# Attention-only batches in another order: scores by pairs of heads, all row maxima first, low-rank products in two row groups and a quad earlier

## The chip, the core and the metric

The kernel runs on one core of one Trainium2 chip. A core has five engines that run side by side, each its own list of instructions in order: TensorE (PE in the tables, its weight loads PEld), VectorE (DVE), ScalarE (ACT), GpSimd (POOL) and SyncE (SP), which here only issues DMAs. They wait for one another on semaphores. The metric is the device time of one execution in microseconds (us).

## The reference

Two layers act on x of shape (8, 256, 512): 8 batches of 256 tokens. Only layer 0 is touched by the change:

```python
# layer 0, attention (16 heads of 32), then an FFN with 4-bit weights and a low-rank addition
xn = rms_norm(x, g_norm) * (1 + scale) + shift          # scale, shift = emb @ W_emb + b_emb
q, k, v = heads(xn @ W_qkv);  q, k = rms_norm(q, g_q), rms_norm(k, g_k)
attn = softmax(q @ k.T * 32 ** -0.5);  o = attn @ v
x1 = o + o @ W_out
w_up = (w_up_q - 7.5) * repeat(w_up_scale, 64)
x2 = relu(x1 @ w_up.T + b_up + x1 @ w_up_lora_a @ w_up_lora_b)
x = x + x2 @ w_down.T + b_down + x2 @ w_down_lora_a @ w_down_lora_b
# layer 1: a scan over 256 tokens (4 stages each), then a mixture of experts
```

## The kernel before

Layer 0 takes the eight batches one after the other. The FFN trails the attention by `LAG` = 3 batches, so batches 0, 1 and 2 are attention only, and batches 3 to 7 carry an FFN of an earlier batch between the attention's instructions (`ffn` is true there). While batches 0 and 1 run, the FFN's weights are made: 16 pieces of 1024 columns, 8 in each batch, by this chain for each piece h. SyncE loads its codes and scales (L238 to L248) into one of two staging buffers, once piece h-2 has left it; VectorE forms (code - 7.5) * scale (`scaled`, L760); TensorE makes the low-rank product a @ b, two matmuls of 16 rows by 512 columns into the banks D[0] and D[1] (`lora`, L555), once piece h-1 has been added; VectorE adds the product (`restore`, L767, two instructions); ScalarE takes the high half in f16 (`weights_high`, L416); GpSimd takes the rest (`weights_low`, L320). In all three batches VectorE also takes maxima over 512-wide parts of layer 1's weights (`part_max`, L772): 12 in batch 1, 36 in batch 2.

A batch has two stretches. In the first, TensorE projects q, k and v (L614, L592) and VectorE scales them (L837, L838); four pieces are made beside it. In the second, four quads c of four heads each go through: scores of the quad into the four banks X[0] to X[3] (L633, one head in each 32-row group of TensorE); row maxima on VectorE (`row_max`, L846, one for a head); exponentials on ScalarE (`exps`, L485, two halves for a head); transposes on TensorE back into the head's bank (L639); a copy to SBUF on VectorE (`turned`, L855). The next quad's scores wait until all four copies are done (L629). Then `weighted(c)` makes the spread inverse sums and the products with v (L652, L657), ScalarE and VectorE gather them (L491, L852). After quad 3 comes the output projection (L686), which waits for the last gather.

VectorE's list in a quad before: the maxima of heads 0, 1 and 2, the gather of the last quad, the copy of head 0, the `restore` of a piece (c > 0), the maximum of head 3, the copies of heads 1 and 2, the reciprocal (L849), the copy of head 3, `scaled` of the next piece. In quad 2 it ends with the next batch's L804, in quad 3 the next batch's L809 stands ahead of the `restore`. The product of the piece for which quad c > 0 has its `restore` stands on TensorE behind `weighted(c-1)`; the eighth piece's stands behind `weighted(3)`, ahead of the output projection.

## Time and profile before

| | |
|---|---|
| median of 3 runs | 2866.41 us (2859.16 to 2866.79) |
| the profiled execution's own time | 2869.92 us |
| its span, first to last instruction | 2868.2 us |
| mean granted TensorE clock | 0.969 of full speed |
| TensorE busy | 2742.7 us (96%) |
| VectorE busy | 1752.6 us (61%) |
| ScalarE busy | 1118.3 us (39%) |
| GpSimd busy | 1345.3 us (47%) |

All times inside the kernel are those of the profiled execution, counted from its first instruction. A granted clock of 1.0 is TensorE's level of 2.4 GHz, 0.5 that of 1.2 GHz; a value between them is a mean over a stretch that had both. An engine's idle time is put down to the instruction whose semaphore came last. A matmul on f32 shows as two records, one for each pass.

### The profile page before, as it was taken

What the parts mean: (1) busy time and instruction counts of PE and PEld (TensorE: products, weight loads), DVE (VectorE), ACT (ScalarE), POOL (GpSimd) and SP (SyncE); (2) the same over time, 40 slices, a digit from 0 to 9 for tenths busy, and PEclk for the clock granted to TensorE, in tenths of its full rate; (3) what the DMA queues carried; (4) which work ended last, traced back from release to release, by engine and by line L of the source; (5) the groups of instructions that cost most, each with busy time, mean ns of one, the idle gap of its engine ahead of it and who ended that gap; (6) DMA issues with size and microseconds to landing.
All of it is one profiled execution on the core that took longest, in us unless ns stands there. A gap on an engine that the chain in (4) does not pass through costs nothing.

```text
span 2868.2 us, 132456 instructions
## 1 busy us (share of the span) xinstructions
PE 2742.7 (96%) x49104; PEld 2436.5 (85%) x49104; DVE 1752.6 (61%) x6310; ACT 1118.3 (39%) x4954; POOL 1345.3 (47%) x3459
## 2 busy tenths in 40 slices
PE   7878999999899989999999999999999999999998
PEld 5545677777799979999998998998999899899987
DVE  3566566655655556666666666666666666666654
ACT  2343435654444333343333333333333333333322
POOL 1120011221156656666665665665666566566600
PEclk9888999999999979999999999999999999999999
DMA  7343344544410014444443443433444344344376
GB/s 231 96 133 121 107 154 149 173 158 150 129 48 4 4 49 129 128 128 134 130 130 125 128 128 125 130 129 125 132 128 128 125 128 129 124 133 128 119 238 202
DMA packets 140246, 364.63 MB, mean 127 GB/s; under 512 B 17536, under 2 KB 27392, under 8 KB 139520
## 3 DMA queue, kind: packets, MB, share of 16 engines
q1 hardware_dynamic: 137504, 355.55, 39.1%
q10 hardware_dynamic: 2560, 6.49, 0.7%
q8 instruction: 135, 2.21, 0.3%
q14 instruction: 47, 0.39, 0.0%
HBM read 327.50 MB, written 34.47 MB: 126 GB/s over the span
## 4 chain that ended last, share of the span: by engine, by line
PE 68%; DVE 1%; issue 1%; ACT 0%; DMA 0%; DVEq 0%; POOL 0%; ACTq 0%; POOLq 0%; SPq 0%
PE pscan L1420 14%; PE pscan L1416 13%; PE pg L1322 12%; PE pd L1373 12%; PE pu L1322 12%; PE pd L1346 2%; PE pg L1334 1%; PE prouter L1334 1%; PE pu L1334 1%; PE prouter L1434 0%; DMA wd<-w_split 0%; PE prouter L1442 0%; DVE state L1549 0%; ACT th L1229 0%; PE pd L1449 0%
## 5 line engine op out<-in xcount | busy, mean ns | idle before, releaser
L1416 PEld LDWEIGHTS pscan<-th,carry 128*128 128x128 f16 x16384 | 561.2, 96 | 38.4 <-ACT th L1229 17.5
L1416 PE MATMUL pscan<-th,carry 128*128 128x8 f16 x16384 | 559.9, 166 | 14.3 <-ACT th L1229 14.1
L1420 PE MATMUL pscan<-th,carry 128*128 128x16 f16 x16384 | 558.7, 169 | 2.4 <-DVE th L1532 1.5
L1420 PEld LDWEIGHTS pscan<-th,carry 128*128 128x128 f16 x16384 | 482.8, 96 | 4.0 <-DVE th L1532 3.5
L1229 ACT ACTIVATE th<-state 128x32 f16<-128x32 f32 x768 | 176.1, 229 | 704.4 <-DVE state L1549 704.4
L1322 PE MATMUL pg<-qh,wgu 128*128 128x256 f16 x3168 | 431.1, 276 | 14.3 <-issue 14.1
L1373 PE MATMUL pd<-hg,wd 128*128 128x256 f16 x3168 | 428.8, 274 | 2.4 <-DMA wd<-w_split 2.4
L1322 PE MATMUL pu<-qh,wgu 128*128 128x256 f16 x3168 | 425.2, 273 | 0.0
L1549 DVE TENSOR_REDUCE state<-pscan 128x32 f32<-128x96 f32 x768 | 197.9, 258 | 271.9 <-PE pscan L1420 267.5
L1322 PEld LDWEIGHTS pg<-qh,wgu 128*128 128x128 f16 x3168 | 296.0, 98 | 54.0 <-issue 15.5
L1322 PEld LDWEIGHTS pu<-qh,wgu 128*128 128x128 f16 x3168 | 293.4, 98 | 32.9
L1373 PEld LDWEIGHTS pd<-hg,wd 128*128 128x128 f16 x3168 | 277.9, 97 | 31.8 <-issue 2.7
L1544 DVE SCALAR_TENSOR_TENSOR pscan<-pscan,lin 128x32 f32<-128x32 f32 x1024 | 204.7, 200 | 127.0 <-DVE pscan L1535 19.9
L1532 DVE TENSOR_TENSOR th<-pact,th 128x32 f16<-128x32 f32 x1024 | 191.2, 187 | 119.3 <-ACT pact L1230 115.1
L1197 POOL TENSOR_TENSOR from_q<-state,carry 128x32 f32<-128x32 f32 x256 | 91.2, 356 | 245.8 <-DVE state L1549 245.8
L1191 POOL TENSOR_TENSOR from_q<-state,carry 128x64 f32<-128x64 f32 x256 | 113.1, 442 | 170.7 <-DVE state L1549 170.7
L1229 ACT ACTIVATE th<-carry 128x32 f16<-128x32 f32 x256 | 58.6, 229 | 342.0 <-DVE carry L1549 333.2
L485 ACT ACTIVATE w_emb<-l0bank,nmax 128x256 f32<-128x256 f32 x256 | 118.7, 474 | 122.1 <-DVE nmax L846 121.7
L1297 ACT ACTIVATE hg<-hp 128x256 f16<-128x256 f32 x264 | 109.8, 416 | 124.3 <-DVE hp L1594 117.5
L326 POOL TENSOR_SCALAR late<-parts_mem 128x512 f16<-128x512 f16 x33 | 51.4, 1559 | 226.8 <-DMA w_split<-late 138.2
L1594 DVE SCALAR_TENSOR_TENSOR hp<-hb,wk,gates 128x256 f32<-128x256 f32 x264 | 141.9, 538 | 18.6 <-DVE hb L1587 7.6
L1535 DVE SCALAR_TENSOR_TENSOR pscan<-pscan,state 128x32 f32<-128x32 f32 x768 | 147.6, 192 | 0.0
(225 smaller groups left out, 4730.8 us busy)
## 6 DMA issues: line engine op xcount, KB each, us to landing
wgu<-w_split SPq DMA_DIRECT2D x264, 512.0 KB, 3.5
wd<-w_split SPq DMA_DIRECT2D x264, 384.0 KB, 3.1
parts_mem<-in_w_tiles SPq DMA_DIRECT2D x159, 256.0 KB, 3.7
w_split<-parts_mem SPq DMA_DIRECT2D x99, 256.0 KB, 2.6
late<-in_w_tiles SPq DMA_DIRECT2D x39, 256.0 KB, 4.0
w_split<-late SPq DMA_DIRECT2D x33, 128.0 KB, 3.0
hid<-in_up_q SPq DMA_DIRECT2D x8, 512.0 KB, 4.3
hid<-in_up_s SPq DMA_DIRECT2D x16, 256.0 KB, 5.2
```

Source lines behind the costliest of these rows:

```text
L485: ins = act.activation(pr[:, h % HPC, qc, :], X[h % HPC][:, qc * T:(qc + 1) * T], ACT.Exp, bias=nmax[:, h % HPC, qc:qc + 1], accum_out=psu ...
L1191: pl.tensor_tensor(ms3[:], rows(state[2][:], 2), c3[:], ALU.mult).then_inc(S["pchain"], 1)
L1229: act.activation(th[:, :, 0, :], v3(src[:]), ACT.Tanh, scale=unit).then_inc(S["th_ready"], 1)
L1322: ins = mm(dst[:, 0:GT], wgu[:, slot, a, w, k, :], qh[:, q, k, :], start=(k == 0 and w == q), stop=(k == NC - 1 and w == 1))
L1373: ins = mm(pd[m // 2][:, (m % 2) * GT:(m % 2 + 1) * GT], wd[:, slot, w, m * P:(m + 1) * P], hg[:, slot, h, :], start=False, stop=False, sk ...
L1416: mm(pscan[:, 0, m * B:(m + 1) * B], clo[:, k, m * P:(m + 1) * P], th[:, k, 0, :], start=(m == 0 and k == 0), stop=False, skip_group_check ...
L1420: ins = mm(pscan[:, 0:2, m * B:(m + 1) * B], chi[:, k, m * P:(m + 1) * P], th[:, k], start=False, stop=(k == NC - 1), skip_group_check=True)
L1532: dve.tensor_tensor(th[:, :, 1, :], v3(t32), th[:, :, 0, :], ALU.subtract).then_inc(S["tl_ready"], 1)
L1535: chain(dve.scalar_tensor_tensor(cub, sq, shift, state[s][:], ALU.add, ALU.mult), False)
L1544: chain(dve.scalar_tensor_tensor(pscan[:, 2, 0:W], cub, -RK[s - 1] / 3, A[u][:, s, :], ALU.mult, ALU.add), False)
L1549: dve.tensor_reduce(nxt[:], pscan[:, 0:3, 0:W].rearrange("p a w -> p w a"), AX.X, ALU.add).then_inc(S["q_ready"], 1)
L1594: dve.scalar_tensor_tensor(hp[:], hb[:], wk[:, 4:5], g, ALU.mult, ALU.mult).then_inc(S["hp_ready"], 1)
```

## The change

In batches 0, 1 and 2 only:

- Scores are made and announced by pairs of heads: the pair of heads 0 and 1 of the next quad waits for the copies of heads 0 and 1 alone, the second pair for those of heads 2 and 3.
- VectorE has a list of its own for these batches (`attention_quad`): four maxima, then `restore` of a piece, then the four copies with the reciprocal behind the third, the gather of the last quad, `scaled` of the next piece. The fourth piece of a batch (`scaled`, `restore`, and the `part_max` that stood behind it) moves from the end of the first stretch into quad 0, behind its maxima.
- The product of piece 4 + c is made behind the transposes of quad c, so that it stands before the `restore` of quad c + 1 needs it, and the eighth piece's stands ahead of `weighted(3)`. The two matmuls of a product read two copies of the factors, at partitions 0 and 64 (or 32 and 96), so they use two different row groups of TensorE. The factors are loaded and scaled twice for it.
- ScalarE takes the four heads' exponentials in a row, with the gather copy and `weights_high` behind them.
- The low half of a batch's eighth piece is made by VectorE, between the two additions that follow the output projection, in place of GpSimd, with a semaphore of its own (`split_end`).

The kernel before and the changed one list their instructions as follows; line numbers are each one's own. VectorE in quad 1 of batch 0, before: L846 is a maximum, L852 the gather, L855 a copy, L767 `restore`, L849 the reciprocal, L760 `scaled`.

```order
L846 TENSOR_REDUCE nmax<-l0bank 128x2 x3
L852 TENSOR_TENSOR late<-l0bank,late 128x256
L855 COPY carry<-l0bank 128x512
L767 SCALAR_TENSOR_TENSOR hid<-hid,fs,l0bank 128x512 x2
L846 TENSOR_REDUCE nmax<-l0bank 128x2
L855 COPY carry<-l0bank 128x512 x2
L849 RECIPROCAL rinv<-psum_e 128x8
L855 COPY carry<-l0bank 128x512
L760 SCALAR_TENSOR_TENSOR hid<-hid 128x1024
```

VectorE in the same quad of the changed kernel: L874 is a maximum, L788 `restore`, L883 a copy, L877 the reciprocal, L880 the gather, L781 `scaled`.

```order
L874 TENSOR_REDUCE nmax<-l0bank 128x2 x4
L788 SCALAR_TENSOR_TENSOR hid<-hid,fs,l0bank 128x512 x2
L883 COPY carry<-l0bank 128x512 x3
L877 RECIPROCAL rinv<-psum_e 128x8
L883 COPY carry<-l0bank 128x512
L880 TENSOR_TENSOR late<-l0bank,late 128x256
L781 SCALAR_TENSOR_TENSOR hid<-hid 128x1024
```

The fourth maximum has moved ahead of the first copy and of `restore`, the gather behind the last copy; the instructions are the same.

TensorE from quad 3 of batch 0 to the output projection, before: L639 are the transposes, L652 and L657 `weighted(3)`, L555 the eighth piece's product, L686 the output projection.

```order
L639 MATMUL l0bank<-ident,w_emb 128x128 x16
L652 MATMUL l0bank<-ident,rinv 32x128 x8
L657 MATMUL l0bank<-carry 32x256 x8
L555 MATMUL l0bank<-late 128x512 x2
L686 MATMUL l0bank<-late,w_out 128x256 x16
```

The same place of the changed kernel, with L654 for the transposes, L559 for the product, L667 and L672 for `weighted(3)` and L704 for the projection.

```order
L654 MATMUL l0bank<-ident,w_emb 128x128 x16
L559 MATMUL l0bank<-late 128x512 x2
L667 MATMUL l0bank<-ident,rinv 32x128 x8
L672 MATMUL l0bank<-carry 32x256 x8
L704 MATMUL l0bank<-late,w_out 128x256 x16
```

The product no longer stands between `weighted(3)` and the projection. In the quads before, it has moved the same way, from behind `weighted(c-1)` to ahead of the next quad's scores.

VectorE from the last scaling of q and k in batch 1 into quad 0, before: L772 is `part_max`, the other lines as above.

```order
L838 TENSOR_TENSOR w_emb<-l0bank,carry 128x256
L760 SCALAR_TENSOR_TENSOR hid<-hid 128x1024
L767 SCALAR_TENSOR_TENSOR hid<-hid,fs,l0bank 128x512 x2
L772 TENSOR_REDUCE xs<-parts_mem 128x1 x3
L846 TENSOR_REDUCE nmax<-l0bank 128x2 x3
L855 COPY carry<-l0bank 128x512
```

The same place of the changed kernel, where L864 is the scaling and L793 `part_max`.

```order
L864 TENSOR_TENSOR w_emb<-l0bank,carry 128x256
L874 TENSOR_REDUCE nmax<-l0bank 128x2 x4
L781 SCALAR_TENSOR_TENSOR hid<-hid 128x1024
L793 TENSOR_REDUCE xs<-parts_mem 128x1 x3
L788 SCALAR_TENSOR_TENSOR hid<-hid,fs,l0bank 128x512 x2
L883 COPY carry<-l0bank 128x512 x3
```

Quad 0's maxima now stand ahead of the fourth piece's work and of the `part_max`, which stand ahead of the first copy instead.

The diff, cut to its core:

```diff
-        lora_up, lora_dn = late[0:R, 0:N + H0], late[32:32 + R, 0:N + H0]
+        lora_up, lora_dn = [late[r:r + R, 0:N + H0] for r in (0, 64)], [late[r:r + R, 0:N + H0] for r in (32, 96)]
...
             for half, factors in enumerate((lora_up, lora_dn)):
-                sp.dma_start(factors, dram["lora"][half]).then_inc(S["lora"], 16)
+                for copy in factors:
+                    sp.dma_start(copy, dram["lora"][half]).then_inc(S["lora"], 16)
...
-                if h >= 2:
-                    sp.wait_ge(S["split"], h - 1)
+                if h >= 2 and (h - 1) % EACH == 0:
+                    sp.wait_ge(S["split_end"], (h - 1) // EACH)
+                elif h >= 2:
+                    sp.wait_ge(S["split"], h - 1 - (h - 1) // EACH)
...
                     for h in piece_at(b, at):
-                        weights_low(h)
+                        if at < EACH - 1:
+                            weights_low(h)
...
                 values()
-                pieces(NC - 1)
...
-                    if c:
+                    if c and ffn:
                         widened(c - 1)
                     relus(ffn_quad[c][0] + ffn_quad[c][1])
                     exps(HPC * c + 2)
                     relus(ffn_quad[c][2])
-                    if c:
-                        pieces(NC + c - 1)
                     exps(HPC * c + 3)
+                    if c and not ffn:
+                        widened(c - 1)
+                    pieces(NC + c - 1)
...
-                        a, bb = lora_up[:, c * P:(c + 1) * P], lora_up[:, col:col + 512]
+                        a, bb = lora_up[i][:, c * P:(c + 1) * P], lora_up[i][:, col:col + 512]
...
+                def scores_by_pairs(c):
+                    for pair in range(2):
+                        if c:
+                            pe.wait_ge(S["d_pt"], b * HEADS + HPC * (c - 1) + 2 * pair + 2)
+                        elif pair == 0:
+                            pe.wait_ge(S["d_qk"], b * NC + NC)
+                        for qc in range(2):
+                            for j in (2 * pair, 2 * pair + 1):
+                                r = DH * j
+                                ins = mm(X[j][:, qc * T:(qc + 1) * T], qk[r:r + DH, c, 0, qc * P:(qc + 1) * P], qk[r:r + DH, c, 1, :], start=True, stop=True)
+                        ins.then_inc(S["p_s"], 1)
...
-                    scores(c)
+                    if ffn:
+                        scores(c)
+                    else:
+                        scores_by_pairs(c)
                     if c:
                         weighted(c - 1)
-                        restored(NC + c - 1)
...
+                    restored(NC + c)
                 weighted(NC - 1)
-                restored(2 * NC - 1)
...
+            def piece_low(h):
+                half, full = split_piece(h)
+                dve.wait_ge(S["a_whi"], h + 1)
+                dve.tensor_tensor(half(1), full, half(0), ALU.subtract).then_inc(S["split_end"], 1)
...
-                    codes_scaled(c)
-                    pieces(c)
+                    if c < NC - 1:
+                        codes_scaled(c)
+                        pieces(c)
                     lows(b, ffn_qk[c])
-                    parts(b, c)
+                    if c < NC - 1 or ffn:
+                        parts(b, c)
...
+                def attention_quad(c):
+                    h = HPC * c
+                    for j in range(HPC):
+                        row_max(h + j)
+                    if c == 0:
+                        codes_scaled(NC - 1)
+                        parts(b, NC - 1)
+                    pieces(NC + c - 1)
+                    parts(b, NC + h)
+                    if c == NC - 1:
+                        normed_input(b + 1)
+                    for j in range(HPC):
+                        turned(h + j)
+                        if j == 2:
+                            inverse(c)
+                    if c:
+                        gathered(c - 1)
+                    codes_scaled(NC + c)
+                    if c == 2:
+                        normed_root(b + 1)
...
+                    if i == 1:
+                        for h in piece_at(b, EACH - 1):
+                            piece_low(h)
```

## Rows read from the trace of the kernel before

**Rows 1.** Busy time by engine in four stretches; last columns clock, DMA share, GB/s.

```profile
64.08:119.39 55.31, 38.28 (x283) 21.76 (x282) 36.09 (x58) 22.41 (x75) 8.85 (x5) 0.80 0.38 110
160.63:218.78 58.15, 38.99 (x282) 22.52 (x280) 37.87 (x61) 22.52 (x75) 9.24 (x5) 0.74 0.36 109
253.03:298.53 45.50, 28.85 (x264) 18.47 (x265) 35.38 (x63) 18.46 (x71) 0.00 (x0) 0.77 0.38 121
309.15:2868.20 2559.05, 2499.44 (x47800) 2276.34 (x47798) 1577.01 (x5997) 1015.48 (x4677) 1306.67 (x3428) 0.98 0.40 126
```

**Rows 2.** Groups by line, 64.08 to 309.15 us: busy, mean ns | idle before, releaser.

```profile
L485 ACT ACTIVATE w_emb<-l0bank,nmax 128x256 f32<-128x256 f32 x96 | 44.3, 474 | 46.1 <-DVE nmax L846 46.1
L639 PE MATMUL l0bank<-ident,w_emb 128*128 128x128 f32 x192 | 34.7, 329 | 42.4 <-ACT w_emb L485 42.4
```

**Rows 3.** Timeline of VectorE, batch 0: start, length, instruction, count, idle before.

```profile
76.21 1.89 DVE L846 TENSOR_REDUCE nmax<-l0bank 128x2 f32<-128x512 f32 x3
79.18 0.42 DVE L852 TENSOR_TENSOR late<-l0bank,late 128x256 f32<-128x256 f32 x1 [1.08 <-ACT late L491]
80.72 1.40 DVE L767 SCALAR_TENSOR_TENSOR hid<-hid,fs,l0bank 128x512 f32<-128x512 f32 x2
82.04 0.68 DVE L846 TENSOR_REDUCE nmax<-l0bank 128x2 f32<-128x512 f32 x1
82.64 1.28 DVE L855 COPY carry<-l0bank 128x512 f32<-128x512 f32 x2
85.48 1.22 DVE L760 SCALAR_TENSOR_TENSOR hid<-hid 128x1024 f32<-128x1024 int32 x1
...
98.92 1.22 DVE L804 TENSOR_TENSOR carry<-xs,rs 128x1024 f32<-128x1024 f32 x1
...
106.32 1.37 DVE L809 TENSOR_SCALAR carry<-carry,amp,ss 128x256 f32<-128x256 f32 x4
```

**Rows 4.** Timeline of TensorE, batch 0, and batch 2's output projection.

```profile
40.45 1.98 PE L555 MATMUL l0bank<-late 16*128 16x512 f32 x4
...
64.08 0.71 PE L633 MATMUL l0bank<-w_emb 32*128 32x256 f32 x6
64.51 0.59 PE L555 MATMUL l0bank<-late 16*128 16x512 f32 x1
...
75.00 1.15 PE L633 MATMUL l0bank<-w_emb 32*128 32x256 f32 x16 [0.79 <-DVE carry L855]
...
111.07 1.11 PE L639 MATMUL l0bank<-ident,w_emb 128*128 128x128 f32 x4 [4.52 <-ACT w_emb L485]
...
115.68 3.78 PE L555 MATMUL l0bank<-late 16*128 16x512 f32 x4
119.39 9.47 PE L686 MATMUL l0bank<-late,w_out 128*128 128x256 f32 x32
...
298.53 7.14 PE L686 MATMUL l0bank<-late,w_out 128*128 128x256 f32 x32 [1.05 <-DVE late L852]
```

**Rows 5.** Timeline of ScalarE in quad 1 of batch 0.

```profile
76.94 0.47 ACT L485 ACTIVATE w_emb<-l0bank,nmax 128x256 f32<-128x256 f32 x1 [2.49 <-DVE nmax L846]
...
77.85 0.47 ACT L485 ACTIVATE w_emb<-l0bank,nmax 128x256 f32<-128x256 f32 x1
...
82.16 1.06 ACT L416 ACTIVATE w_up<-hid 128x1024 f16<-128x1024 f32 x1 [2.09 <-DVE hid L767]
```

**Rows 6.** Timeline of VectorE: batch 1 twice; the last copy of batch 2.

```profile
155.32 1.22 DVE L760 SCALAR_TENSOR_TENSOR hid<-hid 128x1024 f32<-128x1024 int32 x1 [3.62 <-DMA hid<-in_dn_s]
...
164.68 1.86 DVE L772 TENSOR_REDUCE xs<-parts_mem 128x1 f32<-128x512 f32 x3
...
293.95 0.69 DVE L855 COPY carry<-l0bank 128x512 f32<-128x512 f32 x1 [0.50 <-PE l0bank L639]
```

**Rows 7.** Timeline of SyncE: where the load waited for at 155.32 is issued.

```profile
148.43 0.33 SPq L244 DMA_DIRECT2D hid<-in_dn_q  x1
```

**Rows 8.** GpSimd's line L320: ns of one, least, median and most; where.

```profile
L320 POOL TENSOR_TENSOR w_dn<-hid,w_dn x8: 2122/2128/2934, 145.5 to 221.5; 128x1024 f16<-128x1024 f32 x8
```

More of the change, by code:

```diff
@@ L158, in layer0 @@
                  "chain achain seq plseq "
-                 "mm_lora scaled stage split d_bounds g_bounds lora_ok "
+                 "mm_lora scaled stage split split_end d_bounds g_bounds lora_ok "
                  "max_in0 max_in1 max_in2 max_in3 max_in4 max_in5 max_done "
@@ L751, in weight_scales @@
                 link(dve.tensor_scalar(b_up, b_up, swu, None, ALU.mult))
-                dve.wait_ge(S["lora"], 32)
-                dve.tensor_scalar(lora_up[:, 0:N], lora_up[:, 0:N], swu[0:R, :], None, ALU.mult)
-                dve.tensor_scalar(lora_dn[:, 0:H0], lora_dn[:, 0:H0], swd[32:32 + R, :], None, ALU.mult).then_inc(S["lora_ok"], 1)
+                dve.wait_ge(S["lora"], 64)
+                for i in range(2):
+                    up, down = 64 * i, 64 * i + 32
+                    dve.tensor_scalar(lora_up[i][:, 0:N], lora_up[i][:, 0:N], swu[up:up + R, :], None, ALU.mult)
+                    ins = dve.tensor_scalar(lora_dn[i][:, 0:H0], lora_dn[i][:, 0:H0], swd[down:down + R, :], None, ALU.mult)
+                ins.then_inc(S["lora_ok"], 1)
             def scaled(h):
@@ L857, in turned, with quad @@
                         parts(b, NC + h)
-                for c in range(NC):
+                def attention_quad(c):
[18 more added lines that the diff above has]
+                        normed_root(b + 1)
+                def quad(c):
                     h = HPC * c
@@ L868, in batch @@
                         normed_input(b + 1)
-                    if c:
-                        pieces(NC + c - 1)
                     lows(b, ffn_quad[c][0] + ffn_quad[c][1])
@@ L883, in batch @@
                         second(b - LAG, 0)
+                for c in range(NC):
+                    if ffn:
+                        quad(c)
+                    else:
+                        attention_quad(c)
                 gathered(NC - 1)
```

12 lines of the change are left out of this document (6 added, 6 removed).

## The prediction

> **What bounds the kernel now.** I read the busy time by stretch first. From 309.15 us to the end TensorE is busy 2499 of 2559 us, and the change doesn't touch that stretch. In the three attention-only batches it is different: from the first scores to the output projection batch 0 takes 55.31 us, batch 1 58.15, batch 2 45.50, and TensorE is busy 38.28, 38.99 and 28.85 of them, VectorE 36.09, 37.87 and 35.38 [rows 1]. No engine is full there, so a chain of waits sets the pace. The groups by line name it: the transposes (L639) leave TensorE idle for 42.4 us in 64 to 309 us, waiting for ScalarE's exponentials, and the exponentials (L485) leave ScalarE idle for 46.1 us, waiting for VectorE's maxima [rows 2].
>
> VectorE's timeline shows why. In quad 1 of batch 0 the first three maxima start at 76.21, the fourth at 82.04: the gather, a copy and the 1.40 us of `restore` stand ahead of it, and the gather and the copy wait themselves [rows 3]. The head whose maximum is late has its exponentials and its transposes late; in quad 3 TensorE has then waited 4.52 us [rows 4], and the next scores wait for the copy of that head. So the maximum of head 3 is what ends last, and it is late because of the order on VectorE.
>
> **The quads of batches 0 and 1.** Nothing that costs time in a quad is removed; instructions move. With the maxima in front, ScalarE can run four heads in a row at 0.91 us each (76.94 to 77.85 [rows 5]). The last head's transposes are then done about 0.7 + 3.6 + 0.2 + 0.7 = 5.2 us after the first maximum starts (at half clock 5.6: they take 1.11 there [rows 4]). VectorE itself reaches the fourth copy later than that, so its own list becomes the pace. Its lengths [rows 3]: four maxima 4 x 0.63 = 2.5; `restore` 1.4; four copies 4 x 0.64 = 2.6 and the reciprocal 0.2 (an estimate: it has 8 elements for a partition and must be shorter than the gather of 256 with 0.42); gather 0.4; `scaled` 1.2. A plain quad is 8.3 us. These lengths overlap by a few tenths from one to the next; I let that pay for the gaps at the semaphores. Then, for batch 0:
>
> - first scores until the first maximum 1.2 (75.00 to 76.21 [rows 3, 4]);
> - quad 0: no gather, but `scaled` twice, 2.5 + 1.2 + 1.4 + 2.8 + 1.2 = 9.1;
> - quad 1: 8.3; quad 2: 8.3 and L804 with 1.2, 9.5;
> - quad 3 until its last copy: 2.5 + 1.4 + L809 with 1.4 + 2.8 = 8.1 (its gather and `scaled` lie in the tail);
> - tail from the last copy to the projection: batch 2 has no piece there and took 298.53 - 294.64 = 3.9 us [rows 4, 6], with TensorE partly at half clock; I take 3.4.
>
> Sum 39.6 against 55.3: 15.7 us less. The eighth piece's product, 3.78 us long right ahead of the projection [rows 4], is gone from there: the tail now has `weighted(3)`, ScalarE's copy and the gather, and the gather is late next. Batch 1 is the same with three `part_max` of 0.62 [rows 6] moved behind the maxima, 41.5 against 58.15: 16.6 less.
>
> **The quads of batch 2** have no pieces. Quad 0: 2.5, then seven `part_max` 4.3, copies and reciprocal 2.8, two more `part_max` 1.2: 10.8. In quads 1 and 2 ScalarE's four heads are longer than VectorE's list: 0.7 + 3.6 + 0.1, transposes 1.1, copy 0.7, two `part_max` 1.2, gather 0.4 make 7.8, and 9.0 with L804. Quad 3: 2.5 + 0.6 + 1.4 + 2.8 = 7.3. With 1.2 ahead and the tail of 3.9 it is 40.0 against 45.5: 5.5 less.
>
> **The products in two row groups.** One takes 1.98 us now, four passes one after the other [rows 4]. Two by two they take half, about 1.0. Eight of them stand on TensorE's path in the first stretches of batches 0 and 1 (four in each), 8 x 0.95 = 7.6 us at most, and nothing if the passes don't overlap. But there the pieces also wait for their codes: `scaled` waited 3.62 us for a DMA at 155.32 [rows 6]. I take 4.5.
>
> Do two passes overlap? In the trace the last pass of the product starts at 64.51, while six passes of the scores, which stand behind it in the list and use other row groups too, start from 64.08 on [rows 4]. So a row group does not wait for another one's queue, and I keep 1.0. The Trainium skill (TensorE: Matmul & The Clock Gate, Part 3, on what overlaps and what doesn't) says that matmuls start and end strictly in program order. By that rule the second product's first pass could start only with the first one's second, three steps in place of two, about 1.5 us, and the 4.5 would be 2.2. The two rows contradict it for f32 in different row groups.
>
> **Scores by pairs.** Four heads took 1.15 us with four row groups at work [rows 4]. A pair has two: between 0.6 (nothing else limits it) and 1.15 (two groups work at half the rate) for each; I take 0.9. The first pair is issued behind the last transposes and the product; until VectorE comes to the next maximum it has a copy, the gather and `scaled`, 0.7 + 0.4 + 1.2 = 2.3 us. 1.0 + 0.9 and a latency of 0.2 are hidden behind that at full clock. At half clock they are 4.0, 1.7 us too long. The mean clock was 0.80, 0.74 and 0.77 [rows 1]; I charge two of the six such places in batches 0 and 1: 3.4 us lost.
>
> **The projection** took 9.47 us in batch 0, partly at half clock (TensorE had waited 4.52 us before the quad's last transposes), and 7.14 in batch 2 at full [rows 4]. With shorter waits it may gain 2.3 us in each of two batches, or nothing; I take 2.0 in all.
>
> **What I cost at nothing.** Two more loads of the factors and two more scalings, near 30 us: VectorE's first `restore` comes after the first product at 40.45 [rows 4], well after; uncovered they would cost about 2. The low half of the eighth piece on VectorE: not seen there; the nearest row is L804 with as many elements, 1.2 us [rows 3], between the two additions, which lie half a projection, 3.5 us, apart. It waits for ScalarE's high half, which follows the last `restore` and is due 1 us before the first addition. The load behind it on SyncE (piece 9's) starts about 1 us later in the batch than now and is needed only in the next batch's second slot. ScalarE's copy for the gather now stands behind four heads; VectorE wants it only after its copies. `weights_high` too is behind the four heads: that makes a piece's round trip longer, see below.
>
> **Sum:** 15.7 + 16.6 + 5.5 + 4.5 + 2.0 - 3.4 = 40.9 us. Made against the profiled execution, 2869.9 - 40.9 = 2829; that execution was 3.5 us above the median of the runs, so against the median 2866.4 - 41 = **2825 us**.
>
> **Rivals.**
>
> *The order pays in full.* VectorE's list runs without the overlaps I gave away (0.5 us in each of eight quads) and TensorE stays at full clock (3.4 back, 2.6 more in the projections), the products give all they can (3.1): 54 us, 2812. For it: with gaps of 1 to 2 us in place of 4.52 the clock should fall less often. Against it: the loads at 155.32.
>
> *The clock stays as it is in the quads.* All six places pay 1.7 and the projections gain nothing: 41 - 6.8 - 2 = 32 us, 2834. For it: stretch means of 0.74 to 0.80.
>
> *Row groups don't overlap.* The 4.5 are gone and the product of 2.0 ahead of the pair's 0.9 exceeds the cover of 2.3 by 0.8 at six places: 32 us, 2835. Against it the two rows above.
>
> *The saving is given back or doesn't come.* A later TensorE stretch at half clock, or the maxima of batch 3 waiting for loads: within 0.3%, say 2862. Against it: the rest hangs on the end of batch 2 alone.
>
> *Slower: a piece's round trip takes over.* Staging has two buffers, so `scaled` of piece h+2 waits for `restore`, high half, low half and load of piece h. Counted from a quad's first maximum: `restore` done at 3.9; high half behind the fourth head, at 4.6, for 1.06 [rows 5]; GpSimd 2.13 [rows 8]; load 6.9, from 148.43 to 155.32 [rows 6, 7]: ready at 14.8. Two plain quads later less the last instruction it is wanted at 8.3 + 7.1 = 15.4. So 0.6 us is left, and each us of a slower load beyond that is a wait on VectorE in every second quad, with copies and scores behind it. Six quads of batches 0 and 1 have such a piece, so three of them wait, and the gain is lost at 41 / 3, some 14 us of wait in each: a load of 21 us in place of 6.9. At 9 us, as other loads may bring, it costs 5.
>
> **Chances.** Forecast 2825: 0.56, its own range 2816 to 2833; full pay 2812: 0.14; clock 2834: 0.13; row groups 2835: 0.08; given back: 0.06; slower: 0.03. What lies within 0.3% (8.6 us) of 2866.4 can't be told from no change in this measurement. So faster 0.91, same 0.06, slower 0.03. The range takes in the full-pay case near its end, the two cases at 2835 and a slow load on top of one: 2808 to 2847.
>
> **What would show it.** Right: from the first scores to the projection about 40, 41 and 40 us; ScalarE's exponentials four in a row, its idle time ahead of them about 30 us in place of 46.1, TensorE's ahead of the transposes about half of 42.4; VectorE busy nine tenths of these stretches in batches 0 and 1; a product of 1.0 us; no product between `weighted(3)` and the projection. Wrong: `scaled` waiting for DMAs in quads 1 to 3; TensorE's clock still below 0.8 there; a product still of 2 us; or a longer stretch behind batch 2.

## The result and the profile after

The changed kernel took 2831.07 us (median of 4 runs, 2827.64 to 2832.05), the kernel before 2862.78 in the same comparison: ratio 0.9879, 95% interval 0.9864 to 0.9894. That is 31.7 us less by the medians, 35 by the ratio. The forecast was 2825. The profiled execution took 2827.64 us, its span 2825.9.

The same four stretches as in [rows 1], by their own ends:

```profile
60.16:100.18 40.02, 29.80 (x285) 19.82 (x281) 37.25 (x59) 23.11 (x78) 10.63 (x5) 0.91 0.47 139
138.29:180.71 42.42, 32.15 (x280) 21.06 (x280) 38.24 (x62) 21.94 (x75) 9.25 (x5) 0.80 0.47 148
212.30:253.08 40.78, 29.81 (x265) 19.59 (x265) 34.43 (x63) 18.39 (x72) 0.00 (x0) 0.83 0.43 134
263.69:2825.90 2562.21, 2502.56 (x47800) 2277.88 (x47798) 1577.19 (x5997) 1014.44 (x4677) 1301.38 (x3428) 0.98 0.40 126
```

From the first scores to the projection it is 40.0, 42.4 and 40.8 us where 39.6, 41.5 and 40.0 were forecast. VectorE does nearly the same work as before (37.25 us for 36.09 in batch 0) in a stretch 15 us shorter: it is busy 93 and 90% of batches 0 and 1. It has become the pace there, with one exception that follows.

The groups by line from 60 to 264 us, answering [rows 2]; after the bar the idle time ahead of them:

```profile
L488 ACT ACTIVATE w_emb<-l0bank,nmax 128x256 f32<-128x256 f32 x96 | 43.9, 483 | 40.0 <-DVE nmax L874 40.0
L654 PE MATMUL l0bank<-ident,w_emb 128*128 128x128 f32 x192 | 34.8, 327 | 20.9 <-ACT w_emb L488 20.9
...
L874 DVE TENSOR_REDUCE nmax<-l0bank 128x2 f32<-128x512 f32 x48 | 29.7, 680 | 4.0 <-PE l0bank L638 4.0
...
L781 DVE SCALAR_TENSOR_TENSOR hid<-hid 128x1024 f32<-128x1024 int32 x13 | 20.5, 1574 | 4.5 <-DMA hid<-in_dn_s 4.5
```

The transposes wait half as long (20.9 for 42.4 us). ScalarE still waits 40.0 us, but now in one piece ahead of each quad's first exponential and no longer between heads. The last row is a surprise: `scaled` has a mean of 1.57 us, not 1.22.

VectorE's timeline of quad 1 in batch 0, answering [rows 3]:

```profile
68.62 0.64 DVE L883 COPY carry<-l0bank 128x512 f32<-128x512 f32 x1
69.18 2.00 DVE L781 SCALAR_TENSOR_TENSOR hid<-hid 128x1024 f32<-128x1024 int32 x1
71.10 2.47 DVE L874 TENSOR_REDUCE nmax<-l0bank 128x2 f32<-128x512 f32 x4
73.50 1.39 DVE L788 SCALAR_TENSOR_TENSOR hid<-hid,fs,l0bank 128x512 f32<-128x512 f32 x2
74.81 1.28 DVE L883 COPY carry<-l0bank 128x512 f32<-128x512 f32 x2
76.66 0.69 DVE L883 COPY carry<-l0bank 128x512 f32<-128x512 f32 x1 [0.57 <-PE l0bank L654]
...
78.26 1.81 DVE L781 SCALAR_TENSOR_TENSOR hid<-hid 128x1024 f32<-128x1024 int32 x1
80.00 2.47 DVE L874 TENSOR_REDUCE nmax<-l0bank 128x2 f32<-128x512 f32 x4
```

Four maxima in a row, the restore, the copies, with one wait of 0.57 us: 8.9 us from first maximum to first maximum, against 8.3 in the forecast. The difference is the scaling at the quad's end, 1.81 us where 1.2 was charged (2.00 at the end of the quad before).

TensorE at the same place and the projection of batch 0, answering [rows 4]:

```profile
67.25 0.99 PE L559 MATMUL l0bank<-late 16*128 16x512 f32 x2
68.06 0.48 PE L638 MATMUL l0bank<-w_emb 32*128 32x256 f32 x1
68.08 0.59 PE L559 MATMUL l0bank<-late 16*128 16x512 f32 x2
68.38 2.07 PE L638 MATMUL l0bank<-w_emb 32*128 32x256 f32 x15
...
74.29 1.89 PE L534 MATMUL l0bank<-carry,ones 128*128 128x256 f32 x8
...
95.42 1.13 PE L559 MATMUL l0bank<-late 16*128 16x512 f32 x4
97.62 0.64 PE L667 MATMUL l0bank<-ident,rinv 128*32 128x128 f32 x16 [1.07 <-DVE carry L883]
...
100.18 7.14 PE L704 MATMUL l0bank<-late,w_out 128*128 128x256 f32 x32 [1.05 <-DVE late L880]
```

A product is 1.13 us at a granted clock of 1.00 (95.42 to 96.55), where it was 1.98; the last one of a batch has left the place ahead of the projection. A score pass starts at 68.06, ahead of the last two passes of the product that stands before it in the list (68.08). By the rule of the Trainium skill (TensorE: Matmul & The Clock Gate, Part 3), that matmuls start and end in program order, the product would be three steps, an estimate of about 1.5 us; the trace does not agree.

The exception is quad 1. There TensorE makes the sums of squares for the next batch's norm (L534, 1.89 us) between the transposes of heads 1 and 2, and the third copy waits for the transposes behind them: 0.57 us here, 1.41 us in a second profile of the same kernel, in which this quad took 9.5 us with a scaling of 1.22.

### The profile page after: what moved, and what is told of

The parts are those of the page before. It is cut to its first block, busy times and chain, and to the rows that moved or that the text cites. A ratio compares the mean times of both kernels' runs of the same rounds, so it can differ in the third digit from the quotient of the medians.

```text
span 2825.9 us, 132462 instructions
## 1 busy us (share of the span) xinstructions
PE 2720.0 (96%) x49104; PEld 2428.7 (86%) x49104; DVE 1756.9 (62%) x6314; ACT 1115.8 (39%) x4954; POOL 1335.8 (47%) x3457
## 4 chain that ended last, share of the span: by engine, by line
PE 69%; DVE 2%; issue 2%; ACT 0%; DMA 0%; DVEq 0%; POOL 0%; ACTq 0%; POOLq 0%; SPq 0%
PE pscan L1473 14%; PE pscan L1469 14%; PE pg L1375 12%; PE pd L1426 12%; PE pu L1375 12%; PE pd L1399 2%; PE pg L1387 1%; PE prouter L1387 1%; PE pu L1387 1%; PE prouter L1487 0%; DMA wd<-w_split 0%; PE prouter L1495 0%; DVE state L1602 0%; ACT th L1282 0%; PE pd L1502 0%
## 5 line engine op out<-in xcount | busy, mean ns | idle before, releaser
L1640 DVE SCALAR_TENSOR_TENSOR hb<-pu,wk,ha 128x256 f32<-128x256 f32 x264 | 127.6, 484 | 36.3 <-PE pu L1375 21.4
```

The source lines that it names most:

```text
L1640: dve.scalar_tensor_tensor(hb[:], pu[:, 0:GT], wk[:, 1:2], ha[:], ALU.mult, ALU.mult).then_inc(S["hb_ready"], 1)
```

## The experiments

Each kernel was timed beside the kernel before on the same chip, in three groups in which the median of before was 2863.9, 2863.8 and 2864.3 us. So all medians can stand side by side:

| kernel | median, us | ratio to before, 95% interval |
|---|---|---|
| before, again | 2864.4 | 1.0003 (0.9990 to 1.0016) |
| groups_only | 2862.3 | 0.9991 (0.9978 to 1.0004) |
| old_order | 2859.3 | 0.9976 (0.9964 to 0.9988) |
| restore_behind | 2853.5 | 0.9960 (0.9946 to 0.9973) |
| max_behind | 2846.3 | 0.9937 (0.9918 to 0.9956) |
| one_group | 2838.2 | 0.9907 (0.9888 to 0.9927) |
| product_between | 2833.9 | 0.9897 (0.9878 to 0.9916) |
| the changed kernel, again | 2831.6 | 0.9879 (0.9857 to 0.9901) |
| no_pairs | 2831.3 | 0.9885 (0.9868 to 0.9903) |
| not_ahead | 2831.2 | 0.9884 (0.9866 to 0.9902) |
| scaled_late | 2830.9 | 0.9879 (0.9856 to 0.9901) |
| copy_on_scalar | 2825.7 | 0.9864 (0.9844 to 0.9884) |

**The order of VectorE.** Three kernels go back from the changed one step by step. `max_behind` puts the fourth maximum behind the first copy, and so also behind what stands ahead of that copy: the restore, in quads 0 the fourth piece's scaling too, in batch 2 `part_max` instructions. The reciprocal goes behind the last copy:

```diff
-                    for j in range(HPC):
+                    for j in range(HPC - 1):
                         row_max(h + j)
...
                         turned(h + j)
-                        if j == 2:
-                            inverse(c)
+                        if j == 0:
+                            row_max(h + HPC - 1)
+                    inverse(c)
```

> The changed kernel with the fourth row maximum of a quad behind the first copy, as before the change, and nothing else; the restore and the product stay where the change put them. Theory A (the main step of the forecast, the four maxima first): the exponentials of the fourth head start late in all twelve quads and hold the last copy back; with the restore no longer between copy and maximum this costs 0.7 to 1.5 us in each: 8 to 18 us longer, 2839 to 2849. Theory B: the fourth maximum's place matters little now, VectorE is busy all the same in batches 0 and 1 and only batch 2 loses: under 5 us longer. Theory C: it brings back nearly all of the old time: 25 us or more.

Measured: 2846.3, 15 us longer. The three stretches are 48.4, 49.8 and 44.8 us. Theory A's time holds, at its upper end; that the restore still stands ahead of the fourth maximum it left out. VectorE in quad 1 of batch 0:

```profile
73.25 1.89 DVE L874 TENSOR_REDUCE nmax<-l0bank 128x2 f32<-128x512 f32 x3 [0.70 <-PE l0bank L638]
75.06 1.40 DVE L788 SCALAR_TENSOR_TENSOR hid<-hid,fs,l0bank 128x512 f32<-128x512 f32 x2
76.37 0.68 DVE L883 COPY carry<-l0bank 128x512 f32<-128x512 f32 x1
76.97 0.68 DVE L874 TENSOR_REDUCE nmax<-l0bank 128x2 f32<-128x512 f32 x1
```

ScalarE's exponentials of the same quad, first and fourth head, as its timeline shows them:

```profile
73.98 0.47 ACT L488 ACTIVATE w_emb<-l0bank,nmax 128x256 f32<-128x256 f32 x1 [3.76 <-DVE nmax L874]
...
77.68 0.47 ACT L488 ACTIVATE w_emb<-l0bank,nmax 128x256 f32<-128x256 f32 x1 [0.87 <-DVE nmax L874]
```

The second wait is the fourth head's. It shifts every later step of the quad, and the idle time ahead of the exponentials from the first scores to the end of batch 2 is 62.7 us against 40.0. Part of the price may not be the wait itself: the scalings take 1.95 us in the mean there, 0.37 more than in the changed kernel, 4.8 us over thirteen (the reason is below). No run separates the two.

`restore_behind` moves the restore of quads 1 to 3, and in the last quad the input's normalisation, from ahead of that copy to between it and the fourth maximum:

```diff
-                    pieces(NC + c - 1)
+                    if c == 0:
+                        pieces(NC - 1)
...
-                    if c == NC - 1:
-                        normed_input(b + 1)
...
                         turned(h + j)
                         if j == 0:
+                            if c == NC - 1:
+                                normed_input(b + 1)
+                            if c:
+                                pieces(NC + c - 1)
                             row_max(h + HPC - 1)
```

> The changed kernel with two things of VectorE's order put back: the fourth row maximum of a quad behind the first copy, and the restore (with the input's normalisation in the last quad) between that copy and that maximum. The kernel with the first alone took 2846.3 us. Theory A: what stands on VectorE ahead of the fourth maximum delays the exponentials of the fourth head, and by them the last transposes and copies: 1.39 us of restore in six quads of batches 0 and 1, and 1.4 of normalisation in three: 5 to 11 us more, 2851 to 2857. Theory B: VectorE does the same work in another order, and only the maximum's own place counts: within 3 us of 2846. Theory C: the order of VectorE is all of the change: 2862, as before.

Measured: 2853.5, 7.2 us more; theory A's time. But the restore stood ahead of the fourth maximum in `max_behind` too. New is that it stands behind a copy that waits for its transposes, and no longer fills that wait:

```profile
73.89 1.89 DVE L874 TENSOR_REDUCE nmax<-l0bank 128x2 f32<-128x512 f32 x3 [0.70 <-PE l0bank L638]
77.82 0.69 DVE L883 COPY carry<-l0bank 128x512 f32<-128x512 f32 x1 [2.04 <-PE l0bank L654]
78.43 1.40 DVE L788 SCALAR_TENSOR_TENSOR hid<-hid,fs,l0bank 128x512 f32<-128x512 f32 x2
79.74 0.68 DVE L874 TENSOR_REDUCE nmax<-l0bank 128x2 f32<-128x512 f32 x1
```

The fourth maximum starts 5.85 us behind the first (3.72 in `max_behind`), and the fourth head's exponentials start behind a wait of 2.99 us where it was 0.87:

```profile
80.46 0.47 ACT L488 ACTIVATE w_emb<-l0bank,nmax 128x256 f32<-128x256 f32 x1 [2.99 <-DVE nmax L874]
```

`old_order` puts back the rest of the quads' order: the gather ahead of the first copy, ScalarE's widening (its copy for the gather) and high halves between the heads, the product behind the weighted values. The fourth piece stays in quad 0.

```diff
+                    if c:
+                        gathered(c - 1)
...
                         weighted(c - 1)
+                        restored(NC + c - 1)
...
-                    restored(NC + c)
                 weighted(NC - 1)
+                restored(2 * NC - 1)
...
                     exps(HPC * c + 2)
+                    if c:
+                        pieces(NC + c - 1)
                     exps(HPC * c + 3)
```

> The changed kernel with the old order of the quads on three engines: on VectorE three maxima, gathering, first copy, restore, fourth maximum; on ScalarE the widening behind the second head and the split of weights ahead of the fourth; on TensorE the product behind the weighted values. Pairs of heads, the second copy of the factors and the last low half on VectorE stay. Theory A (the forecast's step: with the order go most of 38 us): the time of before less what the row groups alone gave, 2856 to 2863. Theory B: pairs and groups by themselves keep 8 us or more of the gain: 2854 or less. Theory C: the order of TensorE and ScalarE adds nothing to that of VectorE: within 3 us of the kernel with the restore put back.

Measured: 2859.3, another 5.8 us; theory A. Taken back in this order, the ladder from before to after is 5.0 us for the pairs, the row groups, the fourth piece's place and the last low half together, 5.8 for TensorE's and ScalarE's order and the gather, 7.2 for the restore behind the first copy, 15 for the fourth maximum. So 22 of the 33 us hang on how late one maximum starts on VectorE. ScalarE's order, the fourth piece's place and the low half were not tried by themselves.

**The row groups.** `groups_only` is the kernel before with the second copy of the factors and nothing else; `one_group` is the changed kernel with both halves of a product from the first copy:

```diff
-                        a, bb = lora_up[i][:, c * P:(c + 1) * P], lora_up[i][:, col:col + 512]
+                        a, bb = lora_up[0][:, c * P:(c + 1) * P], lora_up[0][:, col:col + 512]
...
-                        a, bb = lora_dn[i][:, hc * P:(hc + 1) * P], lora_dn[i][:, H0:H0 + N]
+                        a, bb = lora_dn[0][:, hc * P:(hc + 1) * P], lora_dn[0][:, H0:H0 + N]
```

> The kernel before, with the low-rank factors loaded twice and the two halves of a product in two row groups; nothing of the order of the quads is changed. Theory A (the forecast): the product goes from 1.98 to about 1.1 us, worth 4.5 us: about 2858. Theory B: in the old order each restore of a quad waits for its product, so that the shorter product also counts there: up to 8 us more, about 2851. Theory C: transfers decide in the first stretches: within 1.5 us of before.

> The changed kernel, with both halves of a low-rank product from the same copy of the factors, hence in one row group; the loads and the scaling of the second copy stay. Theory A (the forecast): a product is 1.98 us again instead of 1.13 at full clock, the eight of the first stretches lie on the path, those of the quads beside other work: 4 to 6 us longer than the changed kernel, about 2836, and the stretch in front of the first scores of batch 0 3 to 4 us longer. Theory B: the first stretches wait for transfers of the pieces, not for products: less than 1.5 us longer. Theory C: overlap is partial and the product 1.5 us in the changed kernel: 2 to 3 us longer.

Measured: alone the groups give 1.6 us (interval from 6 us gained to 1 lost), in the new order their loss costs 6.6 to 8, more than any theory had. The first does not decide between theories A and C. In the second, the first maximum of batch 0 comes 2.0 to 2.8 us later than in two profiles of the changed kernel, that of batch 1, counted from the projection, 1.1 later than in the one whose projection is as long (7.14 us). From first maximum to projection the two batches lose another 2 to 3 us each. TensorE's timeline of `one_group`, the same place as above, and VectorE's next maxima show why:

```profile
70.06 2.93 PE L559 MATMUL l0bank<-late 16*128 16x512 f32 x3
71.94 1.22 PE L638 MATMUL l0bank<-w_emb 32*128 32x256 f32 x2
72.78 1.06 PE L559 MATMUL l0bank<-late 16*128 16x512 f32 x1
73.64 2.09 PE L638 MATMUL l0bank<-w_emb 32*128 32x256 f32 x14
...
75.60 2.49 DVE L874 TENSOR_REDUCE nmax<-l0bank 128x2 f32<-128x512 f32 x4 [1.61 <-PE l0bank L638]
```

The product stands ahead of the scores that VectorE's next maximum needs. In one row group, at a granted clock of 0.50 here, it lasts 3.78 us, and the maximum waits 1.61; in the second profile of the changed kernel, also at 0.50, it lasts 2.07 and no wait shows. In sum VectorE waits 10.9 us for pair scores where it was 4.0; of the difference 3.7 lie ahead of quads 0, behind the last product of the first stretch, and 3.2 in quads 1 and 2.

**The pairs and the product a quad ahead.** `no_pairs` uses one step of sixteen matmuls for all four heads in every batch:

```diff
-                    if ffn:
-                        scores(c)
-                    else:
-                        scores_by_pairs(c)
+                    scores(c)
```

`not_ahead` moves the product back behind the weighted values (the two `restored` edits of `old_order`).

> The changed kernel with the scores of a quad in one step of sixteen matmuls behind the fourth copy, instead of two pairs behind the second and the fourth. In the changed kernel the first maximum starts 1.8 to 2.6 us behind the end of the fourth copy, filled by a gathering and a scaling in batches 0 and 1, and sixteen score matmuls take 2.1 us at full clock and 3.3 at half. Theory A: pairs are worth 0.5 to 1 us in each of six quads of batches 0 and 1 and 1.5 to 2.5 in each of three of batch 2: 7 to 13 us longer than the changed kernel, about 2841. Theory B: the scaling at a quad's end hides the scores in any case: under 4 us longer. Theory C: pairs carry the change: 18 us longer or more.

> The changed kernel with the product of a quad's piece back behind that quad's first weighted values, as before the change, instead of a quad ahead; maxima, copies, restores and scalings stay where the change put them. Theory A: a restore stands behind four maxima (2.5 us) and its product would still be ready, so that the place a quad ahead is worth nothing, and the pair scores even start 1 us earlier: 2828 to 2833. Theory B: a product a quad ahead is what keeps the restore from waiting: six restores wait about 1 to 2 us each, and the last product of a batch stands in front of the projection with 1.1 us: 2838 or more.

Measured: 2831.3 and 2831.2, both the time of the changed kernel. Without pairs the sixteen score matmuls of quad 1 in batch 0 are one row of TensorE's timeline:

```profile
68.80 1.15 PE L648 MATMUL l0bank<-w_emb 32*128 32x256 f32 x16 [0.94 <-DVE carry L880]
```

The two pairs take no longer where nothing comes between them (1.16 us in quad 0 of batch 2 of the changed kernel), and the scaling on VectorE (68.91 to 70.67 us) covers the scores. Theory A was wrong by 7 us and more; B holds. In `not_ahead` the restore does wait, which its group shows (the changed kernel: 0.5 us):

```profile
L789 DVE SCALAR_TENSOR_TENSOR hid<-hid,fs,l0bank 128x512 f32<-128x512 f32 x26 | 18.2, 741 | 6.1 <-PE l0bank L559 5.6
```

From first scores to projection batches 0 and 1 are 2 to 4 us longer (43.6 and 44.5 us). The clock of the projections covers this: they take 7.14 and 7.17 us at a granted clock of 1.00, and 9.43 and 9.46 at 0.75 in the second profile of the changed kernel, so the stretches from a projection to the next first scores are about 2 us shorter (37.4 and 31.8 for 39.6 and 34.2). Against the first profile of the changed kernel, with projections of 7.14 and 7.17 us, batch 2 ends 4.2 us later. So theory B's waits are there, and by the median theory A's time; whether the waits make the projections fast more often was not tried.

**The long scalings.** Five `scaled` in the first profile of the changed kernel take 1.81 to 2.47 us (four in the second). GpSimd's timeline has its subtraction beside each; two of them:

```profile
67.97 2.13 POOL L323 TENSOR_TENSOR w_up<-hid,w_up 128x1024 f16<-128x1024 f32 x1 [5.30 <-ACT w_up L420]
76.86 2.13 POOL L323 TENSOR_TENSOR w_up<-hid,w_up 128x1024 f16<-128x1024 f32 x1 [6.77 <-ACT w_up L420]
```

The first ends at 70.10, the scaling started at 69.18 ends at 71.18; the second ends at 78.99, the scaling started at 78.26 at 80.07. Each ends 1.08 us behind the subtraction, whenever it began, and so do the other three. `scaled_late` moves the scaling to where GpSimd is idle:

```diff
-                    if c == 0:
-                        codes_scaled(NC - 1)
+                    codes_scaled(NC + c - 1)
+                    if c == 0:
                         parts(b, NC - 1)
...
                         gathered(c - 1)
-                    codes_scaled(NC + c)
...
+                if not ffn:
+                    codes_scaled(2 * NC - 1)
```

> The changed kernel, with the scaling of the next piece's codes moved from the end of a quad to behind the next quad's four row maxima, just ahead of the restore. In the changed kernel five of these scalings take 1.81 to 2.47 us instead of 1.22, each where a subtraction of GpSimd (2.13 us) runs beside it, and each ends 1.08 us after that subtraction. Theory A: VectorE's instruction with two operands in SBUF stands still while GpSimd's runs: here GpSimd is idle at the new place, all sixteen scalings take 1.22, and the kernel is 2 to 4.6 us shorter (4.64 us is what the five lost in all). Theory B: the longer scalings only filled the time until the next scores are there: all take 1.22, VectorE waits for scores instead, and the time is that of the changed kernel within 1 us. Theory C: something at the end of a quad other than GpSimd's subtraction slows them, and they stay long at the new place too or others become long.

Measured: 2830.9, no shorter, with two groups of VectorE like this:

```profile
L874 DVE TENSOR_REDUCE nmax<-l0bank 128x2 f32<-128x512 f32 x48 | 29.8, 682 | 8.6 <-PE l0bank L638 8.6
...
L781 DVE SCALAR_TENSOR_TENSOR hid<-hid 128x1024 f32<-128x1024 int32 x13 | 15.8, 1216 | 3.5 <-DMA hid<-in_dn_s 3.5
```

The scalings are 4.7 us shorter in sum (15.8 for 20.5), and VectorE waits 4.6 us longer for scores (8.6 for 4.0). Theory B holds: the lengthened scalings lay beside a wait that was there anyway. `product_between` is `scaled_late` with the product taken from in front of those scores:

```diff
                     if c:
+                        restored(NC + c - 1)
                         weighted(c - 1)
...
-                    restored(NC + c)
+                restored(2 * NC - 1)
                 weighted(NC - 1)
```

> The changed kernel with the scaling of the codes behind the next quad's row maxima, and the low-rank product put between the pair scores of the next quad and the weighted values instead of in front of those pair scores. With the scaling alone moved, VectorE waited 8.6 us in sum for pair scores, and in quads with products the first pair's scores came about 1 us behind the product. Theory A: what sets the quads' pace now is TensorE's order, product first and then the scores that VectorE waits for: without the product ahead the wait for pair scores falls by 3 us or more and the kernel takes 2826 to 2829, 2 to 5 us less than the changed kernel. Theory B: the restore then waits for its product, or the weighted values and transposes come 1 us later, and the time is the same within 1.5 us.

Measured: 2833.9, no gain over `scaled_late`; theory A falls. VectorE's wait for pair scores did shrink, from 8.6 to 5.6 us, but batch 1 took 45.3 us instead of 43.0. It lost them in quad 1: VectorE's copies wait 3.7 us for transposes there (0.7 in `scaled_late`), with TensorE busy without a gap from 151.0 to 163.4 us at a mean granted clock of 0.64 (153.1 to 162.5 us and 0.77 in `scaled_late`). That is one execution of each; what set the clock there stays open, and theory B's time is within the scatter.

**The size of the gain.** Two kernels were run again as they are.

> The changed kernel once more, unchanged, to size the gain. The two profiled executions stand 42.3 us apart (2869.92 and 2827.64), the medians of the first four runs each 31.7 us. Theory A: the profiled execution of before was a long one and that of after a short one, and the stretches by themselves give about 41: then the median ratio here is again 0.987 to 0.990 (28 to 37 us), and the stretches from first scores to projection are 40.0, 42.4 and 40.8 us within 0.3. Theory B: the 42 us are the gain and the first four runs of after were long: ratio 0.985 or less.

> The kernel before once more, unchanged. Its first profiled execution took 2869.92 us, 6 us above the median of its 17 runs (2863.93); the end of batch 2 lay at 309.1 us and the rest took 2559.1, against 2561.5 to 2563.6 in every later profile. Theory A: single executions scatter by several us in the first three batches and by 2 to 3 in the rest, and the forecast was summed on a long one: here the end of batch 2 comes 3 us or more away from 309.1, towards 302 to 306. Theory B: the first profile was typical there and the missing gain is a give-back after batch 2: again 309 within 1 us, and the rest 2559 within 1.

Measured: 2831.6 with ratio 0.9879, and 2864.4. The second profile of before has batch 2's end at 302.8 us, 6.4 earlier than the first, with 53.6, 58.9 and 45.8 us in the three stretches; the second one of the changed kernel has it at 267.8, 4.1 later than the first, with 41.1, 42.3 and 39.0. Behind batch 2 it is 2559.1 and 2563.0 us before, 2562.2 and 2562.1 after. Theory A holds for both kernels, but the stretches of the changed one repeat within 1.8 us, not 0.3.

**A kernel that follows.** Since VectorE is the pace, `copy_on_scalar` gives ScalarE the fourth copy of each quad, in the order of `scaled_late` and with the scores in one step:

```diff
+                        act.wait_ge(S["p_t"], b * HEADS + HPC * (c + 1))
+                        act.activation(prT[:, HPC - 1].rearrange("p a t -> p (a t)"), X[HPC - 1][:], ACT.Copy).then_inc(S["d_pt"], 1)
```

> A kernel that follows from the runs so far: the changed kernel with the scores of a quad in one step, the scaling of codes behind the maxima, and the fourth copy of a quad on ScalarE instead of VectorE, behind the split of weights. Theory A: VectorE is the bound in the quads of batches 0 and 1 (nine tenths busy at 9.0 us a quad); without a copy of 0.64 us and without the 0.6 to 1.25 us that the scalings lose to GpSimd's subtractions a quad takes 8.3 to 8.6: 4 to 7 us less than the changed kernel, 2824 to 2827. Theory B: the round trip of scores, maxima, exponentials, transposes and copies is the bound, and a late copy on ScalarE lengthens it: the same within 1.5 us, or slower by up to 4.

Measured: 2825.7 (2822.6 to 2831.1, 5 runs), against 2826.7 to 2832.5 in nine runs of the changed kernel. The medians are 5 to 6 us apart and the intervals of the two ratios overlap, so it is probably, not surely, the faster one. VectorE's timeline:

```profile
69.19 2.48 DVE L874 TENSOR_REDUCE nmax<-l0bank 128x2 f32<-128x512 f32 x4 [1.16 <-PE l0bank L651]
71.60 1.21 DVE L781 SCALAR_TENSOR_TENSOR hid<-hid 128x1024 f32<-128x1024 int32 x1
...
77.40 2.48 DVE L874 TENSOR_REDUCE nmax<-l0bank 128x2 f32<-128x512 f32 x4 [0.87 <-PE l0bank L651]
...
84.65 2.27 DVE L830 TENSOR_TENSOR carry<-xs,rs 128x1024 f32<-128x1024 f32 x1
86.84 2.47 DVE L874 TENSOR_REDUCE nmax<-l0bank 128x2 f32<-128x512 f32 x4
```

This quad takes 8.2 us in place of 8.9, and VectorE waits about 1 us in it.

## Why the prediction was right, and where its sizes were off

**The quads.** The mechanism is shown. The maximum of the fourth head, late behind other work on VectorE, set the pace; with the maxima first VectorE's own list does, but for quad 1, where TensorE's sums of squares (L534) had no term in the forecast: in batch 2, with 3.34 us of scores at a granted clock of 0.52 ahead of them, this quad took 10.2 and 9.7 us in two profiles where 7.8 was summed. The three forecast lengths hold within 1.5 us, in part by luck: in batch 0 quads 0 to 2 took 28.4 us for 26.9, quad 3 and the tail 10.2 for 11.5. In the two profiles of either kernel these stretches are 159.0 and 158.4 us before, 123.2 and 122.4 after, 35 to 37 us less where 15.7 + 16.6 + 5.5 - 3.4 = 34.4 were summed. The ladder gives the order 28 us (2859.3 less 2831.1 to 2831.6); `old_order`, which keeps the rest of the change, is already 8 to 9 us shorter than before in these stretches (150.3).

**The base of the sum.** This is the step that failed: the sum was made against a single profiled execution and its difference carried over whole to the median. From profile to profile the forecast's 40.9 us is nearly what came, 42.3. But the two profiled executions of before stand 5.6 and 3.2 us above the median of its runs (2864.3), and those of after average 1.7 below theirs. The mean difference of the profiles, 39 us, less 4.4 and 1.7, is the 33 us of the medians. Of the 6.4 us by which the first profile of before was longer up to the end of batch 2, 1.7 lie ahead of the first scores and 3.7 between the first projection and the next scores (the projection took 9.47 us for 7.17), hardly any in the quads. It was luck that the forecast missed by 6 us and not by 8: the median of three runs that the 41 us were taken from, 2866.4, was itself 2.1 us high. Nothing shows that the rest of the kernel gave time back: behind batch 2 the means are 2561.0 and 2562.2 us, inside the scatter of before.

**The products in two row groups.** Right that they overlap: 1.13 us, forecast 1.0. For the first stretches 4.5 us were booked; the groups alone gave about 1.6 in the old order, with 4.5 inside the interval. In the new order their loss costs 3 to 4 us there and 4 to 5 in the quads, because the product was put ahead of the pair scores. The latter was written down as a rival's price, 0.8 us too much at six places if the groups did not overlap; it is what the groups save the new order, and no gain over the old.

**Pairs and half clock.** The pairs were charged 3.4 us and credited with nothing; they are worth nothing measurable, and the charge did not come: the 4.0 us of waiting for pair scores lie ahead of the three quads 0. **The projection's** 2.0 us are not shown: it takes 7.14 or 9.4 us in either kernel, from execution to execution (7.14 and 7.17 in one profile of the changed kernel, at a granted clock of 1.00, 9.43 and 9.46 in the other, at 0.75).

**At nothing.** The factor loads, the low half on VectorE (1.23 us) and the later load did not show in the time. The low half stands behind the wait for the second half of the projection, at 107.36 us in batch 0: it does not fill the 2.8 us for which VectorE idles there, as was meant, but puts the second addition off by 1.1. The scaling was mis-sized, 1.2 us for up to 2.47, 4.6 us in sum; `scaled_late` shows that it cost nothing as things stood. **The rivals:** no scaling waits for a transfer in the quads, so the round trip did not take over. In the first stretches of batches 0 and 1 one does in each (3.68 us at 56.64, 4.53 at 132.98), as before (3.62 us in batch 1, [rows 6]). By its number 2831 is nearer to the rivals of the clock (2834) and of the row groups (2835) than to 2825. The traces speak against both: the products overlap, and no maximum of quads 1 to 3 shows a wait for pair scores; only the gain of the projections, which the first of them denies, is not shown.

**What would show it.** VectorE nine tenths busy, the transposes' wait halved, no product ahead of the projection: as written. ScalarE's wait was forecast at 30 us and is 40.0: when VectorE is the pace ScalarE waits about 3 us ahead of each of twelve quads, which the forecast's own list implied.

## What to carry to other kernels

Where one engine feeds a pipeline of four heads, look at what stands ahead of the last head's first step on that engine: moving it up was worth 22 us, while scores by pairs and a product made a quad earlier were worth nothing measurable. An instruction that waits for nothing can fill the wait of a copy when it stands ahead of it, and adds to it when it stands behind. Once that engine is the pace, a faster step elsewhere pays only where it stands in front of something it waits for, as the product in front of the scores did. Profile twice before a sum is carried over to a median: here one profile was 6 us off in the part that counted.

## What the hardware showed

A VectorE instruction with both operands in SBUF stood still while a subtraction of GpSimd ran that had started before it. The scaling is 1.22 us alone and ended 1.08 us behind the subtraction in all five places where it came second; in `copy_on_scalar` the multiplication of L830, also from two SBUF tiles, took 2.27 us in place of 1.22 [rows 3], beside a subtraction at 83.71 to 85.84, and ended 1.08 us behind it too. The copies (0.64 us) and the gather (0.41), which take at most one operand from SBUF, kept their lengths beside it. Where the scaling came first, in the first stretches, it kept its length and the subtraction took 2.93 us in place of 2.13, as VectorE's and GpSimd's timelines show:

```profile
47.31 1.22 DVE L781 SCALAR_TENSOR_TENSOR hid<-hid 128x1024 f32<-128x1024 int32 x1
47.58 2.93 POOL L323 TENSOR_TENSOR w_up<-hid,w_up 128x1024 f16<-128x1024 f32 x1 [32.07 <-ACT w_up L420]
```

The Trainium skill states it (SBUF — State Buffer, Who interferes with whom): a VectorE instruction with two SBUF inputs contends with a GpSimd instruction that reads SBUF, and the order of issue decides which of the two is blocked. The traces agree. The profile counts the blocked time as busy time of the instruction that waits. In the kernel before no scaling of a quad met a subtraction; the one sign of it was the longest subtraction of [rows 8], 2.93 us, beside a scaling of the first stretch. The forecast did not look at where the new order would put the scalings.
